# Attention layers of a graph network: the rescaled accumulator summed by TensorE, and copied back by ScalarE

## The chip, the cores and the metric

One core of a Trainium2 chip runs the whole program, alone. The metric is the device time of one execution in microseconds (us), the median of several runs. Engines: TensorE (PE; its weight loads are PEld), VectorE (DVE), ScalarE (ACT), GpSimd (POOL), SyncE (SP, here a queue that only starts DMAs).

## The reference, cut to what matters

Four blocks with residuals over 3125 nodes of 256 features and 53,125 edges: an attention layer over the graph (8 heads of 32), a routed feed-forward block, two graph attention (GAT) layers (4 heads of 64), and a small mixture block. The change is in the three attention layers alone. Each of them computes, for every node `i` and head, over the edges that end in `i`:

```
m   = max over edges e of s[e]              # the score of the edge
w   = exp(s[e] - m)
out = sum(w[e] * v[src[e]]) / sum(w[e])
```

In the first layer `s = q[i] . k[src]`; in the GAT layers `s = leaky_relu(a_src[src] + a_dst[i])`, and `v` is the projected row of the source node.

## The kernel before, in words

The nodes are sorted by their number of edges into NT = 25 tiles of P = 128 nodes, one node to a partition. A tile's edges are cut into chunks of ROUNDS = 4 neighbours for each of its 128 nodes. There are 120 chunks in a layer here, in one order given by the table `tile_of`, and a layer is one call of `attend`: name `att` for the first (heads h = 8, qk=True), `gt` twice for the GAT layers (h = 4), called gt0 and gt1 below. The chunks of a tile come one after the other, and the sums are kept the way a streaming softmax keeps them: `acc` (25 tiles x h x (dh + 1) columns, dh = 32 or 64) holds the weighted sum of the values and, in the last column of each head, the sum of the weights; `peak` holds the maximum so far. A new chunk with a higher maximum makes it necessary to multiply `acc` by exp(old peak - new peak) before its own sum is added.

All buffers of a chunk have SLOTS = 4 slots, so a chunk's slot is its number modulo 4. One loop iteration of each engine (a block) is 4 chunks, so there are 30 blocks. Per chunk, in slot k:

- SP (L883, L896) loads the 4 indices of each partition, waits for the rows of the slot and tells DVE (`chunk_ready`).
- POOL (L918) issues 4 indirect DMAs, one for each round, which gather 128 rows each. Before it does so it waits (L913, L915) for the indices and until the chunk that used the slot before, 4 chunks back, has been weighted (`weighted`, and in `att` also `act_weighted`). So POOL can be up to 4 chunks ahead.
- DVE makes the scores (L968 copies the old peak in as a fifth row of scores; L972/L974 and L982/L984), the new peak (L990), and subtracts it from all five rows (L995); L996 keeps the new peak.
- ACT takes the exponential of the five rows at once (L1075) into the weight columns of `wv`. The fifth row of `wv` therefore gets exp(old peak - new peak), the factor for `acc`. In `att` ACT also multiplies two of the four rounds by their weights, in 16 small activations (L1080).
- DVE multiplies the other rounds (two in `att`, all four in `gt`) by their weights (L1001, `weight_chunk`).
- PE sums the four weighted rows into the PSUM bank `part[k]`: 4 matmuls of `wv` rows with the identity (L1098). A matmul of f32 shows as two MATMUL records, so a chunk is x8.
- DVE multiplies `acc` of the tile by the factor, in place (L1009, `rescale`), and adds the PSUM bank to it (L1015, `accumulate`).

The order on DVE is written out by hand in `block_of`, with the chunks skewed. In the pass for chunk j DVE does: scores of j begin, the weighting of chunk j-1, scores of j end, `rescale` of chunk j-2, new peak of j, `accumulate` of chunk j-2, shift of j. `rescale` waits until the last `accumulate` is done (semaphore `added`), `accumulate` waits for `rescaled` and for PE's `part_sum`. In front of the loop `added` is raised by 3 and `rescaled` and `part_sum` by 2, so that chunk j's waits can all be written with n = j + 1. PE waits for `weighted` and `act_weighted` of its chunk only. DVE reads the tile's number from the table with a register load (`tile_at`, L961). Behind the loop DVE does the last two chunks, then divides (L1052 to L1061).

Of the kernel before, what the change touches and what calls it, by code (L numbers as in the profile page):

```python
# [6 lines left out]
ALU, ACT, AX = mybir.AluOpType, mybir.ActivationFunctionType, mybir.AxisListType  # L7

P = 128
N_NODES, N_EDGES = 3125, 53125  # L10
NT = -(-N_NODES // P)
# [3 lines left out]
ROUNDS = 4  # L15
# [812 lines left out]
SLOTS = 4  # L828


def attend(nc, c, g, name, heads, own, own_table, table, width, out_table, qk, bias_row=None):
# [13 lines left out]
    h, dh = heads, D // heads  # L845
    av = dh + 1
# [5 lines left out]
    with Mem(nc, name) as m:  # L852
        rows = m.sb("rows", [P, SLOTS, ROUNDS, width])
        acc = m.sb("acc", [P, NT, h, av])
# [3 lines left out]
        tile_of = m.sb("tile_of", [1, MAX_CHUNKS], I32)  # L858
        score = m.sb("score", [P, SLOTS, ROUNDS + 1, h])
        wv = m.sb("wv", [P, SLOTS, ROUNDS + 1, h, av])  # L860
        recip = m.sb("recip", [P, 2, NT, h])
        part = m.ps("part", [P, SLOTS, 512])
# [10 lines left out]
        def blocks_of(eng):  # L873

            total = eng.value_load(g.first_chunk[0:1, NT:NT + 1], min_val=NT, max_val=MAX_CHUNKS)
            return eng.snap((total + (SLOTS - 1)) // SLOTS)

        with nc.Block() as block:
# [58 lines left out]
            def _(dve):  # L937
# [14 lines left out]
                    dve.wait_ge(state_set, 4)  # L952
                dve.wait_ge(tiles_in, 16)
                dve.sem_inc(weighted, SLOTS)
                dve.sem_inc(added, 3)
                dve.sem_inc(rescaled, 2)
                dve.sem_inc(kept, 1)
                blocks = blocks_of(dve)

                def tile_at(j):  # L960
                    return dve.value_load(tile_of[0:1, bass.ds(j, 1)], min_val=0, max_val=NT - 1)  # L961
# [24 lines left out]
                def raise_peak(k, n):  # L986
                    s = score[:, k, :, :]
                    dve.wait_ge(peaked, n)
                    dve.wait_ge(summed, n)
                    dve.tensor_reduce(new_peak[:, k, 0, :], s.rearrange("p r h -> p h r"), AX.X, ALU.max).then_inc(maxed, 1)  # L990
# [7 lines left out]
                def weight_chunk(k, n):  # L998
                    row, w = rows[:, k, :, :], wv[:, k, :, :, :]
                    dve.wait_ge(exped, n)  # L1000
                    dve.tensor_tensor(w[:, 0:dve_rounds, :, 0:dh], row[:, 0:dve_rounds, v0:v0 + D].rearrange("p r (h d) -> p r h d", d=dh),  # L1001
                                      w[:, 0:dve_rounds, :, dh:dh + 1].to_broadcast([P, dve_rounds, h, dh]), ALU.mult).then_inc(weighted, 1)

                def rescale(k, n, t):


                    a = acc[:, bass.ds(t, 1), :, :].rearrange("p a h f -> p (a h) f")
                    dve.wait_ge(added, n)
                    dve.tensor_tensor(a, a, wv[:, k, ROUNDS, :, dh:dh + 1].to_broadcast([P, h, av]), ALU.mult).then_inc(rescaled, 1)  # L1009

                def accumulate(k, n, t):
                    a = acc[:, bass.ds(t, 1), :, :].rearrange("p a h f -> p (a h f)")
                    dve.wait_ge(rescaled, n)
                    dve.wait_ge(part_sum, n)
                    dve.tensor_tensor(a, a, part[:, k, 0:h * av], ALU.add).then_inc(added, 1)  # L1015

                def block_of(i, first):


                    n = [k + 1 if first else dve.snap(i * SLOTS + (k + 1)) for k in range(SLOTS)]  # L1020
                    t = [tile_at(0 if first else i * SLOTS)]
                    for k in range(SLOTS):
                        one, two = (k - 1) % SLOTS, (k - 2) % SLOTS
                        begin_scores(k, n[k], t[k])
                        if not (first and k < 1):
                            weight_chunk(one, n[k] - 1)

                        if k < SLOTS - 1:
                            t.append(tile_at(k + 1 if first else i * SLOTS + (k + 1)))
                        sum_scores(k, n[k])  # L1030
                        if not (first and k < 2):
                            t_two = t[k - 2] if k >= 2 else tile_at(i * SLOTS + (k - 2))
                            rescale(two, n[k], t_two)
                        raise_peak(k, n[k])
                        if not (first and k < 2):
                            accumulate(two, n[k], t_two)
                        shift_scores(k, n[k], t[k])

                block_of(0, True)
# [4 lines left out]
                last = dve.snap(blocks * SLOTS)  # L1044
                weight_chunk(SLOTS - 1, last)
                for back in (1, 0):
                    t_back = tile_at(last - (back + 1))
                    rescale(SLOTS - 1 - back, last + (2 - back), t_back)
                    accumulate(SLOTS - 1 - back, last + (2 - back), t_back)
                dve.wait_ge(added, last + 3)  # L1050

                dve.tensor_scalar(recip[:, 0, :, :], acc[:, :, :, dh], 1.0e-30, None, ALU.max).then_inc(den, 1)  # L1052
# [15 lines left out]
            @block.scalar  # L1068
            def _(act):
                act.sem_inc(act_weighted, SLOTS)  # L1070
                with act.Fori(0, blocks_of(act)) as i:
                    for k in range(SLOTS):
                        n = act.snap(i * SLOTS + (k + 1))
                        act.wait_ge(shifted, n)
                        act.activation(wv[:, k, :, :, dh], score[:, k, :, :], ACT.Exp).then_inc(exped, 1)  # L1075
                        if act_rounds:
                            act.wait_ge(exped, n)
                            for r in range(dve_rounds, ROUNDS):
                                for e in range(h):
                                    last = act.activation(wv[:, k, r, e, 0:dh], rows[:, k, r, v0 + e * dh:v0 + (e + 1) * dh], ACT.Copy,  # L1080
                                                          scale=wv[:, k, r, e, dh:dh + 1])
                            last.then_inc(act_weighted, 1)
                if not qk:
                    for k in range(groups):
                        act.wait_ge(biased, k + 1)
                        out = own[:, GROUP * k:GROUP * (k + 1), 0:D]
                        act.activation(out, out, ACT.Gelu).then_inc(gelued, 1)

            @block.tensor
            def _(pe):  # L1090
                pe.sem_inc(part_sum, 2)
                with pe.Fori(0, blocks_of(pe)) as i:
                    for k in range(SLOTS):
                        pe.wait_ge(weighted, i * SLOTS + (k + 1 + SLOTS))
                        if act_rounds:
                            pe.wait_ge(act_weighted, i * SLOTS + (k + 1 + SLOTS))
                        for r in range(ROUNDS):
                            last = pe.matmul(part[:, k, 0:h * av], c.ident[:, :], wv[:, k, r, :, :].rearrange("p h f -> p (h f)"),  # L1098
                                             start=(r == 0), stop=(r == ROUNDS - 1))
                        last.then_inc(part_sum, 1)  # L1100


# [893 lines left out]
```

## Time and profile before

| | |
|---|---|
| median of 3 runs | 4901.06 us (4848.03 to 4905.02) |
| the profiled execution | 4902.5 us, its span 4900.4 us |
| busy in the span | PE 2759.9, PEld 1994.3, DVE 2600.0, ACT 1395.4, POOL 1974.0 us |
| mean granted clock of TensorE | 0.736 of full speed |
| loop of `att` | 1393 to 2136 us of the span, 743 us |
| loop of gt0 | 3039 to 3755 us, 716 us |
| loop of gt1 | 3841 to 4567 us, 726 us |

The profile is one execution. The page gives busy time by engine and by group of instructions; the trace behind it can be asked for a stretch of time, and answers with groups, waits or single instructions in order of time. In a timeline each row is: start in us, duration in us, engine, line, operation, output and inputs with their shape, count, and in brackets the idle time of the engine just before it with what ended it. "issue" is idle time for which the profile shows no waited-for event. The PE clock has two levels, 1.2 and 2.4 GHz, and a granted clock of 0.5 is the lower one throughout.

### The profile page before, as it was taken

To read this page: it belongs to the slowest core of one execution; us is meant where nothing else is said; L and a number is where in the kernel's file an instruction comes from. 1 tells how busy PE (TensorE), PEld (TensorE's weight loads), DVE (VectorE), ACT (ScalarE), POOL (GpSimd) and SP (SyncE) were. 2 spreads that over 40 slices of the span, in tenths; PEclk is the share of its full clock that TensorE was granted. 3 is DMA by queue.
4 is the path that set the end of the run, shared out by engine and by line. 5 is a ranking of instruction groups with operands and counts; after the bars stand their busy time and mean duration, and the time that the engine had idled before them with its cause. 6 is when DMAs were issued, how large, how long until landed. Compare 5 with 4: busy or idle time off the path is not lost. (4 is left out here: it accounts for less than half of the span.)

```text
span 4900.4 us, 62986 instructions
## 1 busy us (share of the span) xinstructions
PE 2759.9 (56%) x14559; PEld 1994.3 (41%) x14560; DVE 2600.0 (53%) x6219; ACT 1395.4 (28%) x3757; POOL 1974.0 (40%) x1861
## 2 busy tenths in 40 slices
PE   5385663856534455536599923544444444445289
PEld 3372232722313333324599922333333333333277
DVE  6788977889447777733311123444444344444421
ACT  0433404334136676731144401000002100000134
POOL 0003400034056777740022244676674667666300
PEclk9987755977767767765599966676767666766579
DMA  0240002400356666630222223333332333333200
GB/s 19 70 154 17 0 12 78 154 17 0 108 155 179 180 175 180 180 111 1 71 71 71 71 62 86 88 92 92 88 95 61 85 88 92 86 92 87 71 17 21
DMA packets 269152, 413.89 MB, mean 84 GB/s; under 512 B 98337, under 2 KB 192053, under 8 KB 268721
## 3 DMA queue, kind: packets, MB, share of 16 engines
q0 software_dynamic: 98256, 295.59, 23.1%
q1 hardware_dynamic: 169124, 116.08, 7.9%
q10 hardware_dynamic: 1728, 1.72, 0.1%
q8 instruction: 17, 0.28, 0.0%
q14 instruction: 27, 0.22, 0.0%
HBM read 373.41 MB, written 39.84 MB: 84 GB/s over the span
## 5 line engine op out<-in xcount | busy, mean ns | idle before, releaser
L918 POOL DMA_INDIRECT gt_rows<-h_rows,gt_idx x960 | 998.5, 1040 | 464.8 <-issue 300.2
L1098 PE MATMUL gt_part<-gt_wv,all_ident 128*128 128x260 f32 x1920 | 717.2, 542 | 809.7 <-DVE gt_wv L1001 462.6
L1098 PEld LDWEIGHTS gt_part<-gt_wv,all_ident 128*128 128x128 f32 x1920 | 498.2, 271 | 1028.7 <-DVE gt_wv L1001 521.1
L1098 PE MATMUL att_part<-att_wv,all_ident 128*128 128x264 f32 x960 | 361.5, 543 | 414.0 <-remote 172.0
L918 POOL DMA_INDIRECT att_rows<-kv_rows,att_idx x480 | 506.3, 1055 | 212.4 <-issue 211.8
L1080 ACT ACTIVATE att_wv<-att_rows,att_wv 128x32 f32<-128x32 f32 x1920 | 430.9, 308 | 124.0 <-issue 70.1
L1098 PEld LDWEIGHTS att_part<-att_wv,all_ident 128*128 128x128 f32 x960 | 245.3, 268 | 530.4 <-issue 420.1
L1075 ACT ACTIVATE gt_wv<-gt_score 128x20 f32<-128x20 f32 x240 | 57.1, 238 | 1364.4 <-issue 748.4
L1001 DVE TENSOR_TENSOR gt_wv<-gt_rows,gt_wv 128x1024 f32<-128x1024 f32 x240 | 292.6, 1219 | 0.4 <-ACT gt_wv L1075 0.4
L1015 DVE TENSOR_TENSOR gt_acc<-gt_acc,gt_part 128x260 f32 x240 | 102.0, 425 | 273.2 <-remote 123.0
L608 POOL TENSOR_TENSOR ixcs_off_p<-ixcs_lane_e,all_iota_h 128x2048 f16<-128x2048 f16 x26 | 96.0, 3695 | 323.5 <-issue 214.5
L608 POOL TENSOR_TENSOR ixcd_off_p<-ixcd_lane_e,all_iota_h 128x2048 f16<-128x2048 f16 x26 | 96.4, 3708 | 321.7 <-issue 213.4
L569 DVE TENSOR_SCALAR ixcs_oh_c<-all_iota_h,ixs_col,ixs_val_c 128x512 f16<-128x512 f16 x416 | 216.1, 603 | 14.9 <-PE ixcs_window L594 13.1
L569 DVE TENSOR_SCALAR ixcd_oh_c<-all_iota_h,ixd_col,ixd_val_c 128x512 f16<-128x512 f16 x416 | 216.2, 605 | 14.7 <-PE ixcd_window L594 13.1
L1423 PE MATMUL ex_up<-ex_xe,ex_w 128*128 128x128 f32 x1760 | 207.7, 277 | 12.9 <-DVE ex_xe L1387 12.9
L1423 PEld LDWEIGHTS ex_up<-ex_xe,ex_w 128*128 128x128 f32 x1760 | 206.8, 193 | 16.8 <-DVE ex_xe L1387 13.3
L1432 PE MATMUL ex_down<-ex_w,ex_hid 128*128 128x256 f32 x880 | 199.0, 379 | 0.0
L594 PE MATMUL ixcs_window<-ixcs_oh_c,ixcs_oh_p 128*128 128x512 f16 x416 | 146.2, 501 | 83.5 <-DVE ixcs_oh_c L569 68.5
L594 PE MATMUL ixcd_window<-ixcd_oh_c,ixcd_oh_p 128*128 128x512 f16 x416 | 144.1, 493 | 85.6 <-DVE ixcd_oh_c L569 70.5
L974 DVE TENSOR_TENSOR gt_prod<-gt_rows,gat_own 128x16 f32<-128x16 f32 x240 | 43.1, 180 | 270.0 <-issue 202.0
L972 DVE TENSOR_TENSOR att_prod<-att_rows,at_own 128x1056 f32<-128x1056 f32 x120 | 151.3, 1261 | 56.2 <-issue 34.3
L1432 PEld LDWEIGHTS ex_down<-ex_w,ex_hid 128*128 128x128 f32 x880 | 162.9, 190 | 19.9
(455 smaller groups left out, 5469.9 us busy)
## 6 DMA issues: line engine op xcount, KB each, us to landing
ixbs_parts_bc<-key_parts_s SPq DMA_DIRECT2D x28, 1024.0 KB, 6.6
ixbd_parts_bc<-key_parts_d SPq DMA_DIRECT2D x28, 1024.0 KB, 6.3
ex_w<-in_W SPq DMA_DIRECT2D x16, 1024.0 KB, 7.4
gt_rows<-h_rows,gt_idx POOLq DMA_INDIRECT x960
att_rows<-kv_rows,att_idx POOLq DMA_INDIRECT x480
y_rows<-ex_y POOLq DMA_DIRECT2D x55, 128.0 KB, 2.0
kv_rows<-qv_kv_all SPq DMA_DIRECT2D x5, 1300.0 KB, 6.5
gt_idx<-neighbours_d SPq DMA_DIRECT2D x240, 2.0 KB
```

What stands on the lines that cost most here:

```text
L569: dve.tensor_scalar(oh_c[k % RING][:, :], c.iota_h[:, :], col_e, flat(val_c)[:, bass.ds(i * BATCH + k, 1)], ALU.is_equal, ALU.mult).then_i ...
L594: pe.matmul(window[:, :], oh_p[:, b, k, :], oh_c[k % RING][:, :], start=False, stop=True, skip_group_check=True).then_inc(summed, 1)
L608: pool.tensor_tensor(off_p[:, b, :, :], lane_e[:, bass.ds((i * 2 + b) * BATCH, BATCH)].unsqueeze(2).to_broadcast([P, BATCH, P]), c.iota_h[ ...
L918: pool.indirect_dma_start(out=rows[:, k, r, :], out_offset=None, in_=table, in_offset=bass.IndirectOffsetOnAxis(ap=idx[:, k, r:r + 1], axi ...
L972: dve.tensor_tensor(prod[:, :, :], row[:, :, 0:D + h], q, ALU.mult).then_inc(multiplied, 1)
L1001: dve.tensor_tensor(w[:, 0:dve_rounds, :, 0:dh], row[:, 0:dve_rounds, v0:v0 + D].rearrange("p r (h d) -> p r h d", d=dh), w[:, 0:dve_round ...
L1015: dve.tensor_tensor(a, a, part[:, k, 0:h * av], ALU.add).then_inc(added, 1)
L1075: act.activation(wv[:, k, :, :, dh], score[:, k, :, :], ACT.Exp).then_inc(exped, 1)
L1080: last = act.activation(wv[:, k, r, e, 0:dh], rows[:, k, r, v0 + e * dh:v0 + (e + 1) * dh], ACT.Copy, scale=wv[:, k, r, e, dh:dh + 1])
L1098: last = pe.matmul(part[:, k, 0:h * av], c.ident[:, :], wv[:, k, r, :, :].rearrange("p h f -> p (h f)"), start=(r == 0), stop=(r == ROUNDS ...
L1423: last = pe.matmul(up[:, q // 2, (q % 2) * P:(q % 2 + 1) * P], w1[:, k, h, q * P:(q + 1) * P], xe[:, h, :], start=(h == 0), stop=(h == KC ...
L1432: last = pe.matmul(out, hid[:, q, :], w2[:, k, q, :], start=(q == 0), stop=(q == HC - 1))
```

## The change

The fifth row of `wv` no longer holds only the factor. `rescale` writes its product, `acc` times the factor, into that row instead of back into `acc`, and PE adds it as a fifth row of the chunk's sum. The PSUM bank then holds the new accumulator, and ACT copies it to `acc` (`keep_sum`). DVE's `accumulate` is gone. PE waits for `rescaled` of its chunk in addition; ACT waits for `part_sum`; DVE's `rescale` now waits, through `added`, for ACT's copy. On ACT `keep_sum` of chunk j-2 stands behind the exponential (and in `att` the 16 activations) of chunk j, and ACT reads the tile's number itself.

```diff
@@ attend, DVE @@
-                dve.sem_inc(added, 3)
-                dve.sem_inc(rescaled, 2)
...
                     dve.wait_ge(added, n)
-                    dve.tensor_tensor(a, a, wv[:, k, ROUNDS, :, dh:dh + 1].to_broadcast([P, h, av]), ALU.mult).then_inc(rescaled, 1)
-
-                def accumulate(k, n, t):
-                    a = acc[:, bass.ds(t, 1), :, :].rearrange("p a h f -> p (a h f)")
-                    dve.wait_ge(rescaled, n)
-                    dve.wait_ge(part_sum, n)
-                    dve.tensor_tensor(a, a, part[:, k, 0:h * av], ALU.add).then_inc(added, 1)
+                    dve.tensor_tensor(wv[:, k, ROUNDS, :, :], a, wv[:, k, ROUNDS, :, dh:dh + 1].to_broadcast([P, h, av]), ALU.mult).then_inc(rescaled, 1)
...
-                        if not (first and k < 2):
-                            accumulate(two, n[k], t_two)
...
                     rescale(SLOTS - 1 - back, last + (2 - back), t_back)
-                    accumulate(SLOTS - 1 - back, last + (2 - back), t_back)
@@ attend, ACT @@
                 act.sem_inc(act_weighted, SLOTS)
-                with act.Fori(0, blocks_of(act)) as i:
+                act.sem_inc(added, 3)
+                act.wait_ge(tiles_in, 16)
+                blocks = blocks_of(act)
+
+                def keep_sum(j, k, n):
+
+                    t = act.value_load(tile_of[0:1, bass.ds(j, 1)], min_val=0, max_val=NT - 1)
+                    act.wait_ge(part_sum, n)
+                    act.activation(acc[:, bass.ds(t, 1), :, :].rearrange("p a h f -> p (a h f)"), part[:, k, 0:h * av], ACT.Copy).then_inc(added, 1)
+
+                def block_of(i, first):
                     for k in range(SLOTS):
-                        n = act.snap(i * SLOTS + (k + 1))
+                        n = k + 1 if first else act.snap(i * SLOTS + (k + 1))
...
+                        if not (first and k < 2):
+                            keep_sum(i * SLOTS + (k - 2), (k - 2) % SLOTS, n)
+
+                block_of(0, True)
+                with act.Fori(1, blocks) as i:
+                    block_of(i, False)
+                for back in (1, 0):
+                    keep_sum(blocks * SLOTS - (back + 1), SLOTS - 1 - back, blocks * SLOTS + (2 - back))
@@ attend, PE @@
-                        for r in range(ROUNDS):
+                        pe.wait_ge(rescaled, i * SLOTS + (k + 1))
+                        for r in range(ROUNDS + 1):
                             last = pe.matmul(part[:, k, 0:h * av], c.ident[:, :], wv[:, k, r, :, :].rearrange("p h f -> p (h f)"),
-                                             start=(r == 0), stop=(r == ROUNDS - 1))
+                                             start=(r == 0), stop=(r == ROUNDS))
```

## Rows read from the trace of the kernel before

**Rows 1.** Windows of the three loops: us; PE, PEld, DVE, ACT, POOL busy; clock, DMA share, GB/s.

```profile
1393.00:2136.00 743.00, 361.40 (x960) 245.16 (x960) 516.59 (x1072) 495.72 (x2052) 513.88 (x489) 0.70 0.65 172
3039.00:3755.00 716.00, 355.66 (x960) 247.89 (x960) 316.94 (x1072) 66.78 (x149) 488.07 (x470) 0.69 0.38 89
3841.00:4567.00 726.00, 361.55 (x960) 250.30 (x960) 320.24 (x1072) 66.79 (x149) 491.35 (x471) 0.69 0.38 88
```

**Rows 2.** Groups of gt0's loop: busy us, mean ns, then idle before and releasers.

```profile
L918 POOL DMA_INDIRECT gt_rows<-h_rows,gt_idx x470 | 488.4, 1039 | 214.5 <-issue 142.3 <-DVE gt_wv L1001 72.2
...
L1015 DVE TENSOR_TENSOR gt_acc<-gt_acc,gt_part 128x260 f32 x120 | 51.0, 425 | 132.1 <-DMA at_own<-q_rows,all_order_s 103.9 <-issue 20.0 <-PE gt_part L1098 8.0
```

**Rows 3.** POOL's waits in the loops of gt0 and gt1: us, times, longest.

```profile
POOL gt_rows L918 <- DVE gt_wv L1001: 72.2, 14, 6.6
...
POOL gt_rows L918 <- DVE gt_wv L1001: 80.0, 15, 6.8
```

**Rows 4.** Timeline of gt0, one slow stretch, DVE and POOL.

```profile
3407.43 1.22 DVE L1001 TENSOR_TENSOR gt_wv<-gt_rows,gt_wv 128x1024 f32<-128x1024 f32 x1
...
3423.66 0.43 DVE L1009 TENSOR_TENSOR gt_acc<-gt_acc,gt_wv 128x260 f32 x1 [6.13 <-issue]
...
3429.37 0.43 DVE L1015 TENSOR_TENSOR gt_acc<-gt_acc,gt_part 128x260 f32 x1 [4.13 <-DMA at_own<-q_rows,all_order_s]
...
3430.35 1.22 DVE L1001 TENSOR_TENSOR gt_wv<-gt_rows,gt_wv 128x1024 f32<-128x1024 f32 x1
...
3432.36 0.95 POOL L918 DMA_INDIRECT gt_rows<-h_rows,gt_idx  x1 [6.63 <-DVE gt_wv L1001]
...
3433.35 1.22 DVE L1001 TENSOR_TENSOR gt_wv<-gt_rows,gt_wv 128x1024 f32<-128x1024 f32 x1
```

**Rows 5.** Groups of att's loop: busy us, mean ns, then idle before and releasers.

```profile
L918 POOL DMA_INDIRECT att_rows<-kv_rows,att_idx x469 | 495.8, 1057 | 206.7 <-issue 206.1 <-ACT att_wv L1080 0.3 <-DVE att_wv L1001 0.3
L1080 ACT ACTIVATE att_wv<-att_rows,att_wv 128x32 f32<-128x32 f32 x1904 | 427.4, 308 | 123.9 <-issue 70.1 <-remote 43.1 <-ACT att_wv L1075 7.1
...
L1075 ACT ACT_TABLE_LOAD x29 | 37.2, 1283 | 46.2 <-issue 45.9
```

**Rows 6.** Timeline of gt0: PE, one chunk at each clock level, and DVE.

```profile
3416.09 3.84 PE L1098 MATMUL gt_part<-gt_wv,all_ident 128*128 128x260 f32 x8 [5.36 <-issue]
...
3436.56 1.22 DVE L1001 TENSOR_TENSOR gt_wv<-gt_rows,gt_wv 128x1024 f32<-128x1024 f32 x1
...
3437.83 2.02 PE L1098 MATMUL gt_part<-gt_wv,all_ident 128*128 128x260 f32 x8 [0.57 <-DVE gt_wv L1001]
```

**Rows 7.** All copies by ACT of a 128x256 PSUM tile to SBUF: ns min/median/max.

```profile
L803 ACT ACTIVATE gap_a_t<-gap_turn x75: 375/383/386, 2945.8 to 4684.8; 128x256 f32<-128x256 f32 x75
```

**Rows 8.** Timeline of gt0, the last two chunks.

```profile
3748.67 5.83 PE L1098 MATMUL gt_part<-gt_wv,all_ident 128*128 128x260 f32 x16 [3.65 <-DVE gt_wv L1001]
...
3754.60 0.42 DVE L1015 TENSOR_TENSOR gt_acc<-gt_acc,gt_part 128x260 f32 x1 [0.64 <-PE gt_part L1098]
```

**Rows 9.** Timeline of att, ACT and DVE, from one exponential to the next.

```profile
1614.21 0.27 ACT L1075 ACTIVATE att_wv<-att_score 128x40 f32<-128x40 f32 x1 [0.17 <-DVE att_score L995]
...
1614.52 3.50 ACT L1080 ACTIVATE att_wv<-att_rows,att_wv 128x32 f32<-128x32 f32 x16
...
1617.89 0.42 DVE L1009 TENSOR_TENSOR att_acc<-att_acc,att_wv 128x264 f32 x1
...
1618.70 0.19 DVE L995 TENSOR_TENSOR att_score<-att_score,att_new_peak 128x40 f32<-128x40 f32 x1
...
1618.93 0.28 ACT L1075 ACTIVATE att_wv<-att_score 128x40 f32<-128x40 f32 x1 [0.91 <-DVE att_score L995]
```

**Rows 10.** Timeline of att, one slow stretch, DVE and POOL.

```profile
1751.69 0.21 DVE L968 COPY att_score<-att_peak 128x8 f32 x1 [0.34 <-issue]
...
1763.19 0.17 DVE L968 COPY att_score<-att_peak 128x8 f32 x1
...
1763.33 0.94 POOL L918 DMA_INDIRECT att_rows<-kv_rows,att_idx  x1 [2.90 <-issue]
```

## The prediction, made before the changed kernel was run

> **What bounds the kernel now.** I read the windows of the three loops first, because the diff touches only them: 743, 716 and 726 us [rows 1], 2185 of the span's 4900.4. In none of them is DVE the full engine: it is busy 317 of 716 us in gt0 and 517 of 743 in att [rows 1]. Next the groups. POOL's indirect DMAs are 488.4 us busy plus 142.3 us between two issues, over 470 of them [rows 2]: 1.342 us each, 5.37 us for a chunk of four, 120 x 5.37 = 644 us of gt0's 716. So POOL's issuing paces gt0. The rest is mostly one thing: POOL waits for `weighted`, 14 times for 72.2 us in gt0, 15 times for 80.0 us in gt1 [rows 3], 5.2 us each.
>
> The timeline shows why. About every 49 us the trace has a stretch of some 20 us in which DVE, ACT and SP issue late, behind nothing that the profile names; POOL goes on. In the one quoted, DVE's L1001 stands at 3407.43 and, two chunks on, at 3430.35: 22.9 us, 12.2 more than POOL's 2 x 5.37 [rows 4]. POOL has 4 slots in hand and loses only 5.2 on average, so 7.0 us of the lag is absorbed. It is absorbed because DVE catches up afterwards, one chunk in 3.0 us (3430.35 to 3433.35) [rows 4] against POOL's 5.37. Two numbers therefore rule gt: POOL's 5.37 us per chunk, and how fast the other engines can go when they are behind.
>
> In att, POOL's busy time and 0.30 us between issues make (495.8 + 141) / 469 x 4 = 5.43 us per chunk; 206.7 - 469 x 0.30 = 66 us of its idle are waits [rows 5], and a stretch costs less: DVE's L968 goes from 1751.69 to 1763.19, 6.1 over the pace, and POOL waits 2.6 over the usual 0.3 [rows 10], so 3.5 are absorbed.
>
> **The change part by part.**
> *DVE loses L1015*, 120 x 0.425 = 51 us in a layer [rows 2]. DVE is not the pace, and the work beside it (POOL's issuing) covers it already: 0 us in the steady state. The 132.1 us for which DVE sat idle before L1015 [rows 2] do not go with it: what late thing ends them is in the stretches, and DVE would meet it at the next wait, which is now `added` in front of L1009. Bounds: 0, or a gain of the POOL waits, 152 us in the GAT layers; I take 0, less the one or two issue slots that DVE saves in a stretch, 10 us in all.
>
> *PE gets a fifth row.* A chunk's 8 records take 3.84 us at the 1.2 GHz level and 2.02 us at 2.4 GHz [rows 6]; ten take 4.80 or 2.53. This also adds 120 x 2 records to each layer, by themselves hidden in PE's idle time (356 of 716 us busy) [rows 1].
>
> *The wait for `rescaled`* is what matters. PE used to start chunk j when it was weighted; now it starts when DVE has done `rescale` of j, and nothing of chunk j's five rows may go first. Behind it on ACT comes the copy, and `rescale` of j+1 waits for that copy. A ring is closed, once around per chunk: L1009 0.43, gap to PE 0.05 (L1001's end at 3437.78 by its 1.22 us, PE at 3437.83) [rows 6], PE, gap from PE's end 0.10 (3748.67 + 5.83 to 3754.60) [rows 8], the copy 0.39 (0.383 for 256 columns [rows 7]), gap 0.05. That is PE's time + 1.0: **5.8 us at the lower level, 3.55 at the upper**. What queues behind ACT's wait for `part_sum` is the next exponential; behind DVE's wait for `added` are L990, L995 and so the exponential of that pass. Both are members of the same ring and are counted by it.
>
> *The mix of levels.* The granted clock in gt0 was 0.69 [rows 1]; between 0.5 and 1 that is 38% of the time at the upper level. Chunks per us: 0.38/3.55 + 0.62/5.8 = 0.214, or 4.7 us per chunk. This is under 5.37, so in gt POOL stays the pace between stretches, but the catching up shrinks from 2.4 us per chunk to 0.67. With 120/14 = 8.6 chunks from stretch to stretch and two of them inside one, 6.6 x 0.67 = 4.4 of the 7.0 us are won back before the next. POOL pays the missing 2.6 at each: 14.5 x 2.6 = **38 us per GAT layer, 76 in both**. Bounds: 0 at the upper level; at the lower the ring (5.8) is slower than POOL, (5.8 - 5.37) x 92 + 14 x 7.0 = 138 us per layer.
>
> *ACT in att.* Its own order makes a second ring: exponential 0.31 to the first small activation, 16 of them 3.50 [rows 9], copy 0.39, gap 0.05, then DVE's L1009, L990, L995 and back. From L1009 to L995 were 0.81 us with L1015 between [rows 9], about 0.56 without; L995 to the exponential 0.23. Sum 5.05. One chunk in four also has the table load of 1.283 us [rows 5], now between copy and exponential and beside 0.85 us of DVE: +0.1 to 0.2 on the mean, so 5.2. The other ring gives 5.8 at the lower level (60% of the time at 0.70). Pace: 0.4/5.43 + 0.6/5.8, 5.65 us, + 0.2 x 116 = **25 us**. There is no catching up left (before, DVE's own work was 517/120 = 4.3 us per chunk) [rows 1]: the 3.5 us absorbed in each of some 15 stretches are paid, **50 us**, of which I take 35, as upper-level chunks win a little back. ACT's register load for the tile's number adds some five issues to its 17 per chunk; hidden when ACT waits, but in a stretch ACT's issues are the slow thing: 0 to 25 us, I take **5**.
>
> *The tails.* The last two chunks ran on PE back to back and DVE followed [rows 8]. Now the ring is walked twice with nothing beside it, +6 us a layer by 2 x 5.8 less the 5.8 that stood there: **18 us**.
>
> Sum: 76 + 25 + 35 + 5 + 18 - 10 = +149 us if all hit fully. These overlap: a chunk that is slow by the ring in a stretch is charged twice, and PE, busier per chunk, should see the upper level more. I take 115. The profiled execution (4902.5) is 1.4 us above the median, so no correction: **5015 us**. About 2% (98 us) is what a measurement of this kernel tells from no change.
>
> Two rules of the Trainium skill bear on this, and the numbers above don't use them. The rows show DVE busy 44% of gt0 [rows 1]. The Trainium skill, in "Perfetto Trace Analysis", section "Optimizing Scalar/DVE Operations", lets work move from DVE to Scalar when DVE is saturated; by it the change has nothing to win here, and the trace agrees. The clock rule stands with its rival.
>
> **The rivals.**
> *A. The clock rises (no change within 2%).* PE works longer at a stretch. If that keeps it at the upper level, the ring is 3.55 us, under POOL's pace by 1.8; 6.6 chunks win back all 7.0 us, and gt loses nothing. att keeps 35, tails 12: 4902 + 47, **4950 us**. For it: 0.70 shows the level changing all the time. Against: in steady state PE then works only 2.53 of 5.37 us. The Trainium skill, in "TensorE: Matmul & The Clock Gate", section "What's actually happening", says that the throttled state is the default and that activity releases it, which would favour this rival; the trace, at 0.69 before, does not decide.
>
> *B. It gets faster.* The largest idle on DVE in gt0 stands before L1015 (132.1 us) [rows 2], up to 4 us at a time in the quoted stretch [rows 4]. If that waiting belongs to the instruction's own place and vanishes with it, DVE comes out of each stretch over 4 us earlier, and POOL's 5.2 us waits nearly go: from a saving of 4 us per stretch it decides, 29 x 4 = 116 us, **4786 us**. Against it: in the same stretch L1009 has 6.13 us of the same idle [rows 4].
>
> *C. The ring at the lower level.* Then gt loses 138 each, att (5.8 - 5.43) x 116 + 50 + 5 = 98, tails 18: **5294 us**. For it: PE now waits between chunks for two other engines, which breaks its work up.
>
> **How the numbers follow.** Forecast 0.52, own range 4960 to 5090, two thirds of it over 4999. A 0.30, B 0.07, C 0.11. Slower by over 2%: 0.36 + 0.11 + 0.01 of A = 0.48; faster: 0.05 of B; within 2%: 0.47. The range leaves out B and the far part of C: 4890 to 5150.
>
> **What would show each step.** Right: the idle before L1009 ended by ACT's copy, POOL's waits for `weighted` growing to 7 or 8 us each, rows of x10 at 4.7 to 4.8 and 2.5 us, DVE's passes after a stretch at 3.5 to 5.8 us and not 3.0, att's loop longer by 50 to 80 us. Wrong: passes still near 3.0 us, POOL's waits unchanged (A), the waits gone (B), or a steady pass over 5.5 us in gt (C).

## The result, and the profile after

The changed kernel took 4991.6 us (median of 4 runs, 4969.8 to 5014.1) against 4878.2 us before (4 runs, 4848.0 to 4905.0). The ratio on record is 1.021, 95% interval 1.0166 to 1.0262; the two medians alone give 1.023 (of the four runs before, two took about 4850 us and two about 4903). So the change costs about 2.1%, clear of no change, but whether it is more or less than 2% is open. 5015 us had been forecast. The profiled execution took 4990.55 us, its span 4988.5.

First the windows of the three loops, to be laid beside [rows 1] (us; PE, PEld, DVE, ACT, POOL busy; granted clock, DMA share, GB/s):

```profile
1397.00:2150.00 753.00, 437.64 (x1200) 308.26 (x1200) 472.54 (x942) 494.69 (x2125) 515.60 (x483) 0.74 0.64 168
3059.00:3822.00 763.00, 386.20 (x1200) 277.34 (x1200) 281.36 (x943) 74.17 (x237) 474.50 (x466) 0.75 0.36 83
3915.00:4655.00 740.00, 376.27 (x1200) 271.33 (x1200) 280.67 (x945) 74.88 (x239) 481.21 (x466) 0.78 0.37 86
```

att is 10 us longer from PE's first chunk to the end, gt0 47, gt1 14. DVE has lost 35 to 44 us of busy time per loop and it bought nothing; PE has 240 more records per loop; its granted clock went from 0.69 or 0.70 to 0.74, 0.75 and 0.78. These windows start with PE's first matmul. Since PE now waits for `rescaled`, which DVE issues a pass later, that matmul also comes later: 19 us after the first gather in both GAT layers, 13 before. Measured from the first gather of a layer to the division by the denominators (the first DVE instruction behind the loop), the loops took 757.9, 728.9 and 738.1 us before and 774.7, 782.2 and 758.4 us after. That is 90 us more, all of the 88 by which the span grew. Cut at the last gather of each loop:

| us more than before | att | gt0 | gt1 | sum |
|---|---|---|---|---|
| first to last gather | 11 | 40 | 16 | 67 |
| last gather to division | 5 | 13 | 5 | 23 |

Next the groups of the whole span (busy us, mean ns of one, idle before and what ended it), DVE's rescale, ScalarE's copy and POOL's gathers:

```profile
L1007 DVE TENSOR_TENSOR gt_wv<-gt_acc,gt_wv 128x260 f32<-128x260 f32 x240 | 103.2, 430 | 749.8 <-ACT gt_acc L1068 530.9 <-issue 218.6
L1068 ACT ACTIVATE gt_acc<-gt_part 128x260 f32 x240 | 93.0, 387 | 1108.2 <-PE gt_part L1106 393.6 <-DMA at_own<-q_rows,all_order_s 312.3 <-remote 264.3
L918 POOL DMA_INDIRECT gt_rows<-h_rows,gt_idx x960 | 984.5, 1026 | 533.8 <-issue 302.1 <-DVE gt_wv L999 219.3 <-DVEq L954 12.4
```

The copy takes 0.387 us (0.39 had been taken). DVE's idle time stands before L1007 now, and ScalarE's copy ends 530.9 us of it in the two layers. (Before, it was spread: 273.2 us before L1015, 270.0 before L974.) POOL's idle time has one term that grew: 219.3 us of waiting for `weighted`, against 72.2 + 80.0 [rows 3]. The list of waits says how many there are, here of gt0 and, behind the "...", of gt1 (total us, times, longest):

```profile
ACT gt_acc L1068 <- DMA at_own<-q_rows,all_order_s: 312.3, 30, 20.0
DVE gt_wv L1007 <- ACT gt_acc L1068: 301.5, 80, 16.3
PE gt_part L1106 <- DVE gt_wv L1007: 279.0, 86, 19.0
ACT gt_acc L1068 <- PE gt_part L1106: 199.0, 67, 4.9
POOL gt_rows L918 <- DVE gt_wv L999: 120.0, 21, 7.5
...
POOL gt_rows L918 <- DVE gt_wv L999: 99.3, 21, 8.2
```

The lines of POOL decide the reading. POOL waited 29 times in the GAT layers before, 5.2 us each [rows 3]; it waits 42 times now, and 219.3 / 42 is again 5.2 us. This equal mean misleads, because nine of the 42 waits are under 3 us (two of the 29 before) and 22 are over 6 us (12 before). A better unit is a stretch, counted as one or more neighbouring passes of DVE over 9 us (a pass is the time from one L1001, now L999, to the next): 28 before, 34 now. Per stretch POOL waited 152.2 / 28 = 5.4 us before and 219.3 / 34 = 6.5 us now. So the 67 us are about half more stretches (6 x 5.4 = 33) and half dearer ones (34 x 1.0 = 34). When the changed kernel was profiled again (its time is under the experiments) the same lines were

```profile
POOL gt_rows L918 <- DVE gt_wv L999: 113.7, 19, 8.1
POOL gt_rows L918 <- DVE gt_wv L999: 121.4, 21, 8.2
```

with 36 stretches: 40 waits, and again 6.5 us per stretch. The first line of the list is also worth learning to read: it names a DMA of att's beginning, over 1500 us earlier. Such a releaser means that the profile found nothing: in these 30 cases the copy was simply issued late.

The timeline of one stretch of gt0 after the change (start, us, idle before in brackets; it starts 11 us after POOL had come out of the last one):

```profile
3345.38 2.46 PE L1106 MATMUL gt_part<-gt_wv,all_ident 128*128 128x260 f32 x10 [1.14 <-issue]
3346.23 1.21 DVE L999 TENSOR_TENSOR gt_wv<-gt_rows,gt_wv 128x1024 f32<-128x1024 f32 x1
...
3353.62 0.95 POOL L918 DMA_INDIRECT gt_rows<-h_rows,gt_idx  x1 [0.30 <-issue]
...
3357.14 0.39 ACT L1068 ACTIVATE gt_acc<-gt_part 128x260 f32 x1 [11.24 <-DMA at_own<-q_rows,all_order_s]
3357.67 0.43 DVE L1007 TENSOR_TENSOR gt_wv<-gt_acc,gt_wv 128x260 f32<-128x260 f32 x1 [10.11 <-ACT gt_acc L1068]
3358.16 4.70 PE L1106 MATMUL gt_part<-gt_wv,all_ident 128*128 128x260 f32 x10 [10.32 <-DVE gt_wv L1007]
...
3359.77 1.22 DVE L999 TENSOR_TENSOR gt_wv<-gt_rows,gt_wv 128x1024 f32<-128x1024 f32 x1
...
3361.78 0.95 POOL L918 DMA_INDIRECT gt_rows<-h_rows,gt_idx  x1 [7.21 <-DVE gt_wv L999]
...
3363.51 0.43 DVE L1007 TENSOR_TENSOR gt_wv<-gt_acc,gt_wv 128x260 f32<-128x260 f32 x1 [2.44 <-ACT gt_acc L1068]
...
3364.73 1.22 DVE L999 TENSOR_TENSOR gt_wv<-gt_rows,gt_wv 128x1024 f32<-128x1024 f32 x1
...
3369.86 1.22 DVE L999 TENSOR_TENSOR gt_wv<-gt_rows,gt_wv 128x1024 f32<-128x1024 f32 x1
...
3372.25 0.43 DVE L1007 TENSOR_TENSOR gt_wv<-gt_acc,gt_wv 128x260 f32<-128x260 f32 x1 [1.08 <-issue]
```

Read it as a ring. PE was done with its chunk at 3345.38 + 2.46 = 3347.84. The copy stands at 3357.14, 9.3 us later, then DVE, then PE, each released by the one before it. POOL, which needs none of them at once, went on until its slots ran out at 3354.57, and started again at 3361.78. After the stretch the first passes take 4.96 and 5.13 us (L999 from 3359.77 to 3364.73 to 3369.86), hardly less than POOL's 5.0 to 5.4; before the change they took 3.0 [rows 4]. At 3375 the next stretch has begun. POOL's run without a wait was 3377.41 to 3425.73, 48 us, in the stretch of [rows 4], and is 3361.78 to 3382.03, 20 us, here. In the timeline of POOL in gt0 the runs have a median of 45 us before and 27 after; five of about 20 us follow one another after the change, and except for single fragments of one chunk none before is under 30.

### The profile page after: what moved, and what is told of

It is laid out like the page before. It is cut to its first block and busy times, and to the rows that moved or that the text cites. A ratio compares the mean times of both kernels' runs of the same rounds, so it can differ in the third digit from the quotient of the medians.

```text
span 4988.5 us, 66118 instructions
## 1 busy us (share of the span) xinstructions
PE 2879.6 (58%) x15279; PEld 2106.6 (42%) x15280; DVE 2492.6 (50%) x5859; ACT 1417.6 (28%) x4030; POOL 1967.1 (39%) x1861
## 5 line engine op out<-in xcount | busy, mean ns | idle before, releaser
L1106 PE MATMUL gt_part<-gt_wv,all_ident 128*128 128x260 f32 x2400 | 762.5, 478 | 838.7 <-DVE gt_wv L1007 554.2
L918 POOL DMA_INDIRECT gt_rows<-h_rows,gt_idx x960 | 984.5, 1026 | 533.8 <-issue 302.1
L1106 PEld LDWEIGHTS gt_part<-gt_wv,all_ident 128*128 128x128 f32 x2400 | 548.7, 238 | 1052.5 <-DVE gt_wv L1007 635.2
L1106 PE MATMUL att_part<-att_wv,all_ident 128*128 128x264 f32 x1200 | 437.6, 532 | 355.1 <-DVE att_wv L1007 185.2
L918 POOL DMA_INDIRECT att_rows<-kv_rows,att_idx x480 | 512.9, 1068 | 217.8 <-issue 217.8
L1106 PEld LDWEIGHTS att_part<-att_wv,all_ident 128*128 128x128 f32 x1200 | 308.3, 267 | 484.6 <-DVE att_wv L1007 223.5
L1007 DVE TENSOR_TENSOR gt_wv<-gt_acc,gt_wv 128x260 f32<-128x260 f32 x240 | 103.2, 430 | 749.8 <-ACT gt_acc L1068 530.9
L1068 ACT ACTIVATE gt_acc<-gt_part 128x260 f32 x240 | 93.0, 387 | 1108.2 <-PE gt_part L1106 393.6
L999 DVE TENSOR_TENSOR gt_wv<-gt_rows,gt_wv 128x1024 f32<-128x1024 f32 x240 | 292.3, 1218 | 0.4 <-ACT gt_wv L1074 0.4
L1007 DVE TENSOR_TENSOR att_wv<-att_acc,att_wv 128x264 f32<-128x264 f32 x120 | 52.0, 433 | 220.9 <-ACT att_acc L1068 164.3
```

Of the source, the lines that this page charges most:

```text
L918: pool.indirect_dma_start(out=rows[:, k, r, :], out_offset=None, in_=table, in_offset=bass.IndirectOffsetOnAxis(ap=idx[:, k, r:r + 1], axi ...
L1007: dve.tensor_tensor(wv[:, k, ROUNDS, :, :], a, wv[:, k, ROUNDS, :, dh:dh + 1].to_broadcast([P, h, av]), ALU.mult).then_inc(rescaled, 1)
L1068: act.activation(acc[:, bass.ds(t, 1), :, :].rearrange("p a h f -> p (a h f)"), part[:, k, 0:h * av], ACT.Copy).then_inc(added, 1)
```

## The experiments

Every kernel was compared with the kernel before in runs on the same chip in the same session of measurements. One thing has to be said first, because it sorts all of them: in three sessions the GAT layers had no stretches in which DVE, ScalarE and SP issue late, and the kernel before took 4693.3, 4694.5 and 4698.0 us; in two sessions they had, and it took 4898.0 and 4901.0. So there are quiet sessions and sessions with stretches.

### Quiet sessions: what the change costs without the stretches

The expectations of the first four runs were written for a machine with stretches, as in the two profiles. Their session had none. So they say nothing of how the stretches act, and all the more plainly what is left of the change without them.

**Late wait.** The changed kernel, but PE waits for the rescaled row only before the fifth row, so that four rows are outside the ring.

```diff
-                        pe.wait_ge(rescaled, i * SLOTS + (k + 1))
                         for r in range(ROUNDS + 1):
+                            if r == ROUNDS:
+                                pe.wait_ge(rescaled, i * SLOTS + (k + 1))
```

> The change as it is, but PE waits for rescaled only in front of the fifth row; the other four rows go as soon as the chunk is weighted. Ring theory (a ring of rescale, all five rows, copy sets the speed of catching up): only two records of the fifth row stay in the ring, 1.0 us at the lower clock and 0.5 at the upper, so the ring is 1.5 to 2.0 us and DVE's passes behind a slow stretch are 3.0 us again, not 3.6; POOL's waits for weighted fall from 120 and 99 us in the GAT loops to 70 to 85 each; ratio to before 1.003 (1.000 to 1.008). Rival, extra PE work or ACT's part is the cost wherever the wait stands: passes stay at 3.6 us or more, ratio 1.02.

Measured: 4696.6 us, ratio 1.0001 (0.9974 to 1.0028). In its groups POOL has no wait for `weighted` at all in the two GAT layers:

```profile
L918 POOL DMA_INDIRECT gt_rows<-h_rows,gt_idx x960 | 1005.3, 1047 | 314.4 <-issue 301.0 <-DVEq L954 12.4 <-DMA gt_idx<-neighbours_d 0.9
L1007 DVE TENSOR_TENSOR gt_wv<-gt_acc,gt_wv 128x260 f32<-128x260 f32 x240 | 102.4, 427 | 34.2 <-issue 27.3 <-ACT gt_acc L1068 6.6
```

**The change in the GAT layers alone, and in att alone.** `attend` stands twice in the file, once as before and once as changed, and each layer calls one of them.

```diff
-            attend(nc, c, g, "gt0", ...
+            attend_gat(nc, c, g, "gt0", ...
```

> The change in the two GAT layers alone; the first attention layer is as before. The changed kernel's own loops were 53 and 20 us longer in its profile: ratio 1.015 (1.011 to 1.019). By the prediction's terms (76 us and 12 of tails) 1.018. If most of the loss were in the first layer: under 1.007.

> The change in the first attention layer alone. By the prediction's terms (25 + 35 + 5 + 6 = 71 us): ratio 1.014. By the loops of the two profiles (775 against 758 us): 1.003 (1.001 to 1.006), passes never under 5.0 us because the second ring over ACT's 16 small activations holds them there.

Measured: GAT alone 4709.1 us, 1.0027 (1.0007 to 1.0048); att alone 4698.8, 1.0016 (1.0000 to 1.0032). Together 0.4%, some 20 us, of the 2.1%; the whole changed kernel was not run in a quiet session. From gather to division the GAT loops were 665.5 and 666.4 us changed, and 660.8 and 660.6 unchanged (in the att-only kernel): 5 and 6 us more, of which the tails are 6 and 3. att was 700.8 us changed; unchanged it took 708.0 us in the GAT-only kernel and 698.6 in a later quiet one, so no cost in att can be told from the spread.

**A fifth row without a ring.** The kernel before, with a fifth matmul per chunk that multiplies by zeros.

```diff
-                        for r in range(ROUNDS):
-                            last = pe.matmul(..., c.ident[:, :], wv[:, k, r, ...], start=(r == 0), stop=(r == ROUNDS - 1))
+                        for r in range(ROUNDS + 1):
+                            last = pe.matmul(..., (c.ident if r < ROUNDS else c.zeros)[:, :], wv[:, k, r % ROUNDS, ...], start=(r == 0), stop=(r == ROUNDS))
```

> The kernel before with a fifth matmul per chunk whose weights are zeros, so that it adds nothing and waits for nothing new: ten records per chunk, no ring. Ring theory: PE's extra work is hidden, ratio 1.000 (0.997 to 1.003), and the granted clock rises as it did in the changed kernel, to about 0.75. Rival, PE's own work costs: 360 chunks x 0.5 to 1.0 us = 180 to 350 us if none is hidden, 1.005 or more if some is, because L1015 then waits longer.

Measured: 4694.2 us, 0.9997 (0.9975 to 1.0018), mean granted clock 0.783. PE's two more records per chunk cost nothing.

**ScalarE's part alone.** The kernel before, plus on ScalarE, per chunk, the register load of the tile's number, the wait for PE's sum, and a copy of a constant that nobody waits for.

```diff
+                def idle_copy(j, k, n):
+                    t = act.value_load(tile_of[0:1, bass.ds(j, 1)], ...)
+                    act.wait_ge(part_sum, n)
+                    act.activation(copied[:, k, :], c.iota_f[:, bass.ds(t, 1)].to_broadcast([P, 115]), ACT.Copy)
```

> The kernel before, with only ScalarE's part of the change added: per chunk the register load of the tile's number, the wait for PE's sum and a copy (115 columns of a constant into a scratch tile, about 0.25 us in place of 0.39), for which nobody waits. DVE still adds the sum itself, PE has four rows, there is no ring. ScalarE theory, in its form that the number of ScalarE's issues in a stretch makes the exponentials late: ratio to before 1.01 to 1.025, POOL's waits for weighted rising by 15 us or more in a GAT loop. Ring theory, or the ScalarE theory in the form that it is rescale's wait for the late copy that costs: 0.997 to 1.005. If the chip shows no stretches (before near 4693 us), 1.000 to 1.003 by all.

Measured: 4699.3 us, 1.0007 (0.9997 to 1.0018), against a kernel before at 4694.5. The session was quiet, so this tells nothing of ScalarE's share in a stretch, which was the question.

**DVE puts the sum back.** The changed kernel with the ring kept, but without ScalarE in it: DVE adds zeros to the sum, right before the next rescale.

```diff
+                def keep_sum(k, n, t):
+                    dve.wait_ge(part_sum, n)
+                    dve.tensor_tensor(acc[... t ...], part[:, k, 0:h * av], c.zeros[:, 0:1].to_broadcast(...), ALU.add).then_inc(added, 1)
-                    act.activation(acc[... t ...], part[:, k, 0:h * av], ACT.Copy).then_inc(added, 1)
```

> The changed kernel, but the sum goes back into the accumulator on DVE and not on ScalarE: DVE adds zeros to it (the same form of instruction as L1015 of before, about 0.43 us) one pass later, right before the rescale of the next chunk. PE's fifth row and its wait for the rescaled row stay. ScalarE is as before the change. Two theories of the 2% that the change costs on a chip with late-issue stretches. Ring: PE's chunk stands between two rescales, so the loops catch up more slowly whoever copies: then this kernel keeps the loss, ratio to before 1.015 to 1.03, and POOL's waits for weighted in the GAT loops stay near 100 us or more each. ScalarE: the loss comes from ScalarE's copy and its register instructions, which issue late in a stretch, with rescale waiting behind them: then it goes away, ratio 0.995 to 1.007, POOL's waits back near 75 us. If the chip shows no stretches (before near 4693 us), both expect 1.000 to 1.006, and the run tells nothing of the theories.

Measured: 4757.8 us, 1.0131 (1.0110 to 1.0152), in the same quiet session. That is outside what both theories expected of one. About half of the 63 us is att, 732.0 us against 701.5 in the kernel with ScalarE's part alone, and 24 us are the two GAT loops, 20 of them in the tails. A row says where in att:

```profile
L918 POOL DMA_INDIRECT att_rows<-kv_rows,att_idx x480 | 539.4, 1124 | 148.6 <-issue 143.7 <-ACT att_wv L1081 4.6 <-DMA att_idx<-neighbours_s 0.3
```

POOL's indirect DMAs in att took 1.124 us each, 1.066 in the other kernel of the session (511.9 us for the same 480). 27.5 of the 30 us are POOL's own indirect DMAs; no wait was added. Why they took longer is open. It isn't a busier DVE: in these loops DVE was busy 572 us here and 584 in the other kernel. In the GAT layers POOL's mean stayed at 1.055 against 1.052. So the next kernel has the DVE copy in the GAT layers alone.

> The GAT layers changed, with DVE and not ScalarE putting the sum back (by adding zeros, 0.43 us, right before the next rescale); att as before. ScalarE theory: with stretches (before near 4880 us) POOL's waits for weighted in gt0 and gt1 together stay near 150 us, as in the kernel before, the two loops are at most 30 us longer in sum (13 us each by the tails, which the kernel with DVE copying everywhere has shown), and the ratio to before is 1.000 to 1.008. Ring theory: the waits are 200 us or more, the two loops 60 us or more longer in sum, the ratio 1.012 to 1.02. Without stretches (before near 4694 us), both expect 1.003 to 1.008 from the tails, and nothing is told apart.

Measured: 4713.8 us, 1.0034 (1.0020 to 1.0049), before 4698.0. Again a quiet session, and it repeats what was expected of one.

### Sessions with stretches

**The changed kernel again, and lags added by hand.** In three kernels DVE also sums 22 x 512 elements that nobody needs, in each second block of the GAT layers: 11.88 us, 14 times per layer, so that DVE falls behind as in a stretch. One is the kernel before with it, one the changed kernel, one the changed kernel with the late wait.

```diff
-                with dve.Fori(1, blocks) as i:
-                    block_of(i, False)
...
+                else:
+                    with dve.Fori(0, 14) as i:
+                        block_of(i * 2 + 1, False)
+                        dve.tensor_reduce(lagged[:, :], ..., AX.X, ALU.add)
+                        block_of(i * 2 + 2, False)
+                    block_of(29, False)
```

> The changed kernel unchanged, beside the kernel before on one chip. In the last four profiles DVE's slow stretches were absent, the kernel before took 4693 us, and the parts of the change cost 0.3% (GAT layers) and 0.2% (first layer). Catch-up theory (the loss is the catching up that the ring slows down, so without stretches there is little): ratio 1.005 (1.002 to 1.008) where the profile has no stretches, 1.02 where it has them. Rival, the 2.1% is a steady cost of the change: 1.015 or more on any chip.

> The kernel before with a lag made on purpose: in the two GAT layers DVE sums 22 x 512 elements, which nobody uses, about 12 to 13 us, at the beginning of every second block (14 times a layer); this is the 12.2 us lag of the prediction's stretch, and only DVE has it. By the prediction's arithmetic 7.0 of 12.2 are absorbed by POOL's slots and 5.2 are lost: 14 x 5.2 = 73 us per layer, ratio 1.03 (1.02 to 1.04), DVE's passes behind a lag at 3.0 us.

> The changed kernel with the same lag. Catch-up theory: passes behind a lag at 3.6 us (upper clock) to 5.8 us, so that part of the 7.0 us is not won back before the next lag: 1 to 3 us more lost per lag, 28 lags, ratio to the kernel before 1.04 to 1.055, and 30 to 80 us above the lagged kernel before (of which about 20 are there without lags). Rival, the lag costs both the same because 8 chunks are enough to catch up: at most 25 us above the lagged kernel before.

> The changed kernel with the wait for rescaled moved in front of the fifth row, with the same lag. Catch-up theory with the ring as its cause: passes behind a lag near 3.0 us again, the time within 10 us of the lagged kernel before. Rival, the ACT copy or the rows themselves slow the catching up: as slow as the lagged changed kernel.

Measured, one session, before 4898.0 us:

| kernel | us | ratio to before |
|---|---|---|
| changed, again | 4998.8 | 1.0205 (1.0171 to 1.0239) |
| before, with lag | 5089.0 | 1.0390 (1.0350 to 1.0430) |
| changed, with lag | 5172.5 | 1.0540 (1.0495 to 1.0585) |
| changed, late wait, with lag | 5164.4 | 1.0544 (1.0510 to 1.0577) |

The change repeats at 2.05%. On top of the lag it costs 83 us, less than without it (101). And the late wait, which takes four of PE's five rows out of the ring, gives back nothing that can be told from the spread of the runs. POOL's waits for `weighted` in the two GAT layers, first of the kernel before with the lag:

```profile
POOL gt_rows L920 <- DVE gt_wv L1003: 367.1, 34, 17.8
```

of the changed kernel with the lag:

```profile
POOL gt_rows L920 <- DVE gt_wv L1001: 434.7, 55, 17.4
```

and of the one with the late wait:

```profile
POOL gt_rows L920 <- DVE gt_wv L1001: 427.5, 52, 18.7
```

The total rises by 68 and 60 us. Here the number of waits says little by itself, since their mean falls from 10.8 to 7.9 and 8.2 us: in the lagged kernel before, an added lag and a stretch close to it were often one wait (13 waits are over 14 us), and in the other two they are mostly two waits (1 and 3 are over 14 us).

Did the late wait bring the fast catching up back? It did. The first three passes behind a long one take, by their medians, 9.4 us together in the lagged kernel before, 12.0 in the changed one with the lag and 9.4 in the one with the late wait. If slow catching up alone were the cause, this last kernel would have had waits like the lagged kernel before. It had 427.5 us of them, so that theory isn't the whole. A part may still be due to it: in the profiled executions the two GAT loops together were 60 us longer than in the lagged kernel before with the early wait, and 35 with the late one. But runs of one of these kernels differ by 30 to 65 us, and the medians of the whole time differ by 8.

**DVE puts the sum back in the GAT layers, again**, this time with stretches (before 4901.0 us).

> The same kernel as the last one, since no run of it has met the late-issue stretches yet. With stretches (before near 4880 us) the ScalarE theory expects 1.000 to 1.008, the GAT loops together at most 30 us longer than before, POOL's waits for weighted near 150 us in both; the ring theory 1.012 to 1.02, the loops 60 us or more longer, the waits 200 us or more. Without stretches (before near 4694 us) it repeats 1.003.

Measured: 5007.7 us, 1.0201 (1.0167 to 1.0235). The list of waits, gt0 and then gt1:

```profile
POOL gt_rows L1190 <- DVE gt_wv L1272: 146.3, 26, 7.4
...
POOL gt_rows L1190 <- DVE gt_wv L1272: 145.8, 23, 7.4
```

292 us in 49 waits and 46 stretches, 6.35 us per stretch. The loops took 788.7 and 793.6 us, 115 us more in sum than the 728.9 and 738.1 of the kernel before, where the ScalarE theory allowed 30. So the loss does not need ScalarE's copy: with DVE in its place the GAT layers alone lose as much as the whole change did, and the same kernel costs 0.34% in a quiet session. A doubt remains. This kernel issues more on DVE: 2846 instructions of all kinds in gt0, register ones included, against 2576 before, 2.25 per chunk, and in a stretch each costs time. The changed kernel issues 241 fewer on DVE and 687 more on ScalarE (1016 against 329). So a ring that includes whatever is late in a stretch, and the mere number of issues, both fit this run; the late wait with the lag fits only the second, or a ring in which PE's part doesn't matter.

## Why the prediction came out right, and where it did not

**The time.** 5015 forecast, 4991.6 measured, inside the range and inside the likeliest case's own (4960 to 5090). Half of that agreement is luck, as the terms show.

**The ring's sizes: right.** Ten records take 4.70 and 2.46 us (4.80 and 2.53 taken). Once around at the lower level is 3357.67 to 3363.51, 5.84 us (5.8); at the upper, two steps of L1007 in the timeline of gt0:

```profile
3341.29 0.43 DVE L1007 TENSOR_TENSOR gt_wv<-gt_acc,gt_wv 128x260 f32<-128x260 f32 x1 [2.66 <-issue]
...
3344.89 0.43 DVE L1007 TENSOR_TENSOR gt_wv<-gt_acc,gt_wv 128x260 f32<-128x260 f32 x1 [1.08 <-issue]
```

3.60 us (3.55); 79 of the steps of L1007 in the GAT layers are within 0.05 of this. This is what "a ring is closed" can give: durations and gaps from rows of before, added up, were right to 2%.

**DVE's L1015: right.** Its going bought nothing, and the idle time that stood before it stands before L1007 (749.8 us in both layers). Rival B, in which it would vanish, did not happen.

**GAT: the sum near, the mechanism half right.** 76 us was forecast and 56 measured between first and last gather: 67 by POOL's waits, less 14 by POOL's own DMAs (984.5 against 998.5 us). The step "with 120/14 = 8.6 chunks from stretch to stretch" took the number of stretches as given and charged each of the 14.5 per layer with 2.6 us more. Measured were 1.0 us more for each, and more of them: 14 and 14 in the two layers before, 19 and 15 after, 18 and 18 in the repeated run, 23 and 23 with DVE copying. What the profile of the changed kernel was to show, "POOL's waits for `weighted` growing to 7 or 8 us each", came true for some only: 22 of 42 are over 6 us, the longest 8.2. The size per stretch was too large in part because the clock rose: by the step's own formula, with rings of 3.60 and 5.84 us, an estimate for a clock of 0.75 is 0.9 us missing per stretch, and for 0.78 it is 0.1. That the number stays was taken without a reason. The spacing of the stretches is not independent of the kernel: in gt0 after the change they start down to 26 us apart, while none in gt0 of before stood closer than 41 and in gt1 one pair at 28.

**The catching up: right as an observation, not shown as the cause.** Passes after a stretch did slow down as forecast (4.96 and 5.13 us in the quoted one, then 3.73; the first three together have medians of 10 us before and 13 after). But in the late-wait kernel with lags they were fast again and the waits stayed. What makes the next stretch come sooner was not found. It isn't only that POOL has fewer slots in hand: from POOL's start again to the last multiplication of DVE before the next long pass there are 30 us before and 21 after (medians of both GAT layers), and from there to POOL's stop 13 and 11. The experiment that could separate the number of issues from the waiting, ScalarE's part alone, met no stretches, and the unaltered late wait was not run with stretches either. This stays open.

**att: mis-sized, the largest error.** 25 us for the pace, 35 for the stretches and 5 for the register loads; measured 11 between first and last gather. The ring through ScalarE was right, as two rows of the timeline of att show:

```profile
1624.55 0.43 DVE L1007 TENSOR_TENSOR att_wv<-att_acc,att_wv 128x264 f32<-128x264 f32 x1 [0.86 <-ACT att_acc L1068]
...
1629.58 0.43 DVE L1007 TENSOR_TENSOR att_wv<-att_acc,att_wv 128x264 f32<-128x264 f32 x1 [0.84 <-ACT att_acc L1068]
```

5.03 us (5.05). What failed is what was built on it. "Pace: 0.4/5.43 + 0.6/5.8" let each chunk at the lower level be a whole 5.8; PE's chunks in att were often not all at one level (4.00 and 3.93 us stand in the timeline beside 2.49 and 4.77), and the granted clock rose to 0.74. The passes did grow, from a median of 5.8 us to 6.0, but they vary and POOL's slots even them out; in the quiet session the changed att took 678 us from first to last gather, as the unchanged one did (680 to 689), so this term measured nothing. And "the 3.5 us absorbed in each of some 15 stretches are paid": POOL's idle time in att is the row

```profile
POOL att_rows L918 <- issue: 217.8, 480, 7.5
```

against 211.8 counted the same way before, 6 us more and not 35. The other part of the 11 us is POOL's own DMAs, 512.9 us against 506.3.

**The tails: right.** 18 us forecast, 23 measured from last gather to division, 5, 13 and 5; gt0's holds a stretch. It is also the part that remains without stretches, 6 and 3 us in the two GAT layers.

**Rival A** had its premise in part: the granted clock rose from 0.69 to 0.75 and 0.78, but PE did not stay at the upper level. The rise made each stretch cheaper than forecast; it did not make GAT lose nothing, as the rival said. **Rival C**, a steady pass over 5.5 us, did not occur: passes outside the stretches stayed at POOL's pace.

The discount from 149 to 115 us, made for overlaps, was close to what was wanted (the ratio of 1.0214 is 105 us at 4901; the medians differ by 113, the two profiled executions by 88). It repaired att's terms, which were too large, and not the overlap for which it was made.

## What to carry to other kernels

An instruction saved on an engine that is not the pace is worth nothing: 51 us of DVE per layer bought no time here. What came with it, a wait that ties three engines into a ring and some more instructions, cost little where the ring, added up, is shorter than the pace, 0.4% in quiet sessions, and 2.1% as soon as members could be late by 10 us; which of the two costs it is not shown. When a profile shows disturbances at regular intervals, do not take their number as given while working out the cost of each: ask what starts and what ends them, count them again afterwards, and look at single waits before believing a mean. And compare a kernel with its predecessor on the same chip in the same session, since the time between two sessions differed here by twice what the change did.

## What the hardware showed that had not been expected

The late-issue stretches come and go for the same kernel. One and the same chip ran the kernel before in 4898.0 us in one session and in 4694.5 us in the next, 4.2% less; the traces of the other kernels of that second session have none of POOL's waits in the GAT layers. What decides it is not known. The change's cost went with it: about 0.4% in quiet sessions by its two parts added up, 2.1 and 2.05% otherwise.

The stretches seem to end when POOL stops. In the quoted one POOL's last gather ended at 3354.57 and DVE's L1007 came at 3357.67, 3.1 us later; in [rows 4] DVE's L1015 comes at 3429.37, and POOL's last gather before it was this row of before:

```profile
3424.78 0.95 POOL L918 DMA_INDIRECT gt_rows<-h_rows,gt_idx  x1 [0.30 <-issue]
```

It ended at 3425.73, 3.6 us before. In the five regular stretches after the change this distance was 3.0 to 3.2 us each time. It fits the counts above, 28 stretches with 29 waits before and 34 with 42 after, but it was only read from timelines: no run made POOL pause on purpose. POOL's unbroken row of indirect DMAs can't be the whole reason for a stretch, though. In the quiet sessions POOL issued through whole GAT loops without a wait, and no stretch came. A kernel that paced POOL would be the next thing to try.

In att of the kernel in which DVE copies everywhere, in a quiet session, POOL's indirect DMAs took 1.124 us on average in place of 1.066, which is 27.5 of the 30 us by which the loop was longer; in the unchanged att of two other quiet profiles they took 1.063 and 1.081. DVE was not busier there, and the reason is not known.
